# Graph layer, attention and experts on one core: degrees from VectorE's sums, attention stored from GpSimd, transposes moved into the next product

## The chip, the cores and the metric

The program runs on one core of a Trainium2 chip. The metric is the device time of one execution in microseconds, of which the median over several runs is taken.

## What is computed

1250 nodes with 1024 features and 40000 edges go through a layer norm, then side by side through a two-layer graph convolution and a linear-attention block; the sum with the input goes through a second layer norm and a mixture of eight experts. Cut to the parts that matter here:

```python
x = x + positional_encoding
deg = segment_sum(ones, dst) + 1.0
dinv = deg ** -0.5
h = gcn_conv(x, W1, b1)                     # x @ W1, gathered by src, summed by dst, scaled by dinv[src]*dinv[dst]
h = relu((h - mean) * rsqrt(var + eps) * gamma + beta)
h = relu(gcn_conv(h, W2, b2))
attn = linear_attention(xn, Wq, Wk, Wv, proj) @ Wo + bo
x = x + h + attn
x = x + experts(layernorm(x))
```

## The kernel before, in words

Every engine has its own program, and all of them walk the same list ORDER, made by steps(). A key of the list, such as ("O", 3), is one unit of work; each engine does its share of it and skips keys that don't concern it. Semaphores psum_full, act_done and dve_done count the units that TensorE, ScalarE and VectorE have finished; an engine that needs a unit waits for its number. SP issues nearly all DMAs, also in the order of ORDER, so a wait for one holds back all behind it. GpSimd issues the additions into adj_d and, late in the program, the experts' gathers and scatters.

float32 products are made of float32r parts: a matrix is split in a high and a low part (ScalarE copies the high part, VectorE subtracts), and three products are summed. Two PSUM areas, slot0 and slot1, take the results in turn; free_slot() makes TensorE wait until the last user of a slot has been read.

The stages around the change, in order:

- **The adjacency counts.** During the attention stage groups of 500 edges are turned into small blocks of counts, which GpSimd adds into adj_d in DRAM, one addition after the other. When the last is in, GpSimd raises adj_complete (L834).
- **Eight blocks O 0 to 7** (slab_product, L1785): the output projection of the attention, 72 products of 418 columns for each block of 128 output features. ScalarE evicts a block to mixt with the bias (L958). Inside the next block, after the third of eight steps kt, TensorE transposes mixt by ten transposes (mix_transposes, L1712, key OT); VectorE copies the result to mixn (L1444); SP stores mixn to mix_d as 1250 rows of 512 B (key OT, L595). mixn has one buffer for the first seven blocks, so the copy of block f waits for the store of block f - 1. OT f stands in the slot that O f + 2 needs. Between them SP loads adj_d in three thirds of 418 columns (key RL and RP 0, tile raw, 125 rows of 4180 numbers each, two buffers), and ScalarE and VectorE copy each third, one half each, into adj as float32r (RP 0 to 2, L896 and L1302), at O 3, 4 and 5.
- **DG** (L1842), between O 5 and O 6: 30 products of ones with adj (ten row tiles by three thirds) give the degree of every node on all 128 partitions. VectorE takes the maximum with 1, ScalarE the root (L951), VectorE the reciprocal and a Newton step (DN, L1310), and ten small transposes (DT) give the same with nodes on partitions.
- **Z 1**: eight blocks of 60 products with adj (L1857), the first layer's aggregation.
- **Eight blocks H 0 to 7** (slab_product again): the first layer's product. ScalarE evicts with the bias to htmp (L989, semaphore h_biased), VectorE takes mean and variance, ScalarE applies them with the relu (L994). Then key HT: ten transposes of htmp (L1874), ScalarE copies to hout, SP stores it to h_d. HT f - 1 comes after H f in the list, as a unit of its own.
- **Z 2** with h_d, the second product (N), and the experts.

Of the kernel before, what the change touches and what calls it, by code (L numbers as in the profile page):

```python
# [17 lines left out]
F32R = mybir.dt.float32r  # L18
# [5 lines left out]
ALU = mybir.AluOpType  # L24
# [4 lines left out]
T = 125  # L29
# [63 lines left out]
def steps():  # L93
# [55 lines left out]
    for layer in (1, 2):  # L149
# [14 lines left out]
        for f in range(KD if layer == 1 else 0):  # L164
            o += with_split(("H", layer, f))
            if f == 4:
                o.append(("ZP", 2, 0))
            if f:
                o.append(("HT", f - 1))
# [22 lines left out]
INNER |= {("FT", i) for i in range(NT - 1)}  # L192
# [84 lines left out]
def build(nc, x, src_cols, dst_cols, dst_groups, slabs, wv, w1, w2, wr, proj, feat_rows, consts, turns, tie,  # L277
          iota, keys, eye, pe, blank, before, list_blank, tokens, expert_at, b2_rows, out):
    ctx = ExitStack()
    with ctx:  # L280
# [28 lines left out]
        def at(name, off, shape, dt=F32):  # L309
            return nc.alloc_sbuf_tensor_at(name, shape, dt, offset=base + off)  # L310
# [38 lines left out]
        mixt = at("mixt", R + 75776, [128, NP])  # L349

# [240 lines left out]
        def _(sp):  # L591
# [68 lines left out]
            for k in ORDER:  # L660
# [78 lines left out]
                elif k[0] == "OT":  # L739
                    f = k[1]  # L740
                    sp.wait_ge(dve_done, DVED[k])
                    spread(mix_d.rearrange("(j p) (f c) -> f p j c", p=T, c=128)[f], mixn[f // (KD - 1)][:, :, :],
                           mix_stored[f // (KD - 1)])
# [51 lines left out]
        def _(pool):  # L795
# [38 lines left out]
            pool.sem_inc(adj_complete, 1)  # L834

# [301 lines left out]
        def _(dve):  # L1137
# [111 lines left out]
            for k in ORDER:  # L1249
# [48 lines left out]
                elif kind == "RP":  # L1298
# [3 lines left out]
                    dve.tensor_copy(adj[:, NT // 2:, o:o + CW], raw[h % 2][:, :, NT // 2:].rearrange("p d j -> p j d")  # L1302
                                    ).then_inc(dve_done, 1)
# [306 lines left out]
        def _(ten):  # L1610
# [94 lines left out]

            def mix_transposes(f):
# [63 lines left out]
            def slab_product(k, ps):  # L1770
# [5 lines left out]
                for kt in range(KD):  # L1776
# [11 lines left out]
                    if kt == 2 and k[0] == "O" and k[1]:  # L1788
                        mix_transposes(k[1] - 1)
                    if kt == 1 and k[0] == "Q" and k[1]:  # L1790
                        attention_product(("AT", k[1] - 1, 1))
# [8 lines left out]
            for k in ORDER:  # L1800
# [35 lines left out]
                if kind == "DG":  # L1836
# [3 lines left out]
                    for j in range(NT):  # L1840
                        for q in range(3):
                            mm = ten.matmul(ps[:, 512 * q:512 * q + CW], ones_r[:T, :], adj[:, j, CW * q:CW * q + CW],  # L1842
                                            start=(j == 0), stop=(j == NT - 1))
# [26 lines left out]
                elif kind == "HT":  # L1870
                    src_t = htmp[k[1] % 2]
                    ten.wait_ge(act_done, ACTED[("H", 1, k[1])])
                    for j in range(NT):
                        mm = ten.transpose(ps[:T, 128 * j:128 * j + 128], src_t[:, T * j:T * j + T], ident[:, :])  # L1874
# [238 lines left out]
```

## Time and profile before

| | |
|---|---|
| Runs | 1512.24, 1513.09, 1516.08 us; median 1513.09 us |
| Profiled execution | span of 1512.1 us; its time isn't listed apart from the runs |
| TensorE | busy 1420.6 us, 94%, 7718 products |
| VectorE, ScalarE | 852.9 us (56%), 533.1 us (35%) |
| GpSimd | 185.5 us (12%) |
| DMA | 194.34 MB, 129 GB/s; q1 (issued by SP) 32.8% of 16 engines, q0 (issued by GpSimd) 17.5% |
| Mean granted TensorE clock | 0.983 of full speed |

Times count from the start of the span. In a row of the chain of waits stand start, length and what held the end back; in a timeline row start, length, engine, line, instruction and in brackets the idle time ahead of it with its releaser; in a DMA row packets, MB and the time of the packets as a share of 16 engines.

### The profile page before, as it was taken

How to read it: one execution, taken by the hardware profiler on the slowest of the kernel's cores; microseconds unless marked ns; L12 is line 12 of the kernel's file. 1: busy time of each engine (PE TensorE's matmuls, PEld its weight loads, DVE VectorE, ACT ScalarE, POOL GpSimd, SP SyncE). 2: the span in 40 equal slices, each digit the busy share in tenths (PEclk: the TensorE clock that was granted, in tenths of full speed). 3: DMA queues.
4: the chain of work that ended last, by engine and by line, in shares of the span. 5: the costliest groups of instructions: out<-in, count | busy, mean ns of one | idle time of the engine just before them, and what ended most of it. 6: DMA issues, size and time to landing. Idle time of an engine off the chain costs nothing.

```text
span 1512.1 us, 20042 instructions
## 1 busy us (share of the span) xinstructions
PE 1420.6 (94%) x7718; PEld 1305.8 (86%) x7718; DVE 852.9 (56%) x1563; ACT 533.1 (35%) x621; POOL 185.5 (12%) x182
## 2 busy tenths in 40 slices
PE   6999899999999999899999999999999849999995
PEld 5888889998998899899999999999788648888884
DVE  7464677777777787733656323355567744443340
ACT  4233344354344444423122133322111234544441
POOL 0111210110100101000000000000001442223311
PEclk9999999999999999999999999999999959999998
DMA  9765433232431434868353033221655578887863
GB/s 307 238 163 113 74 52 77 44 79 51 71 76 30 98 72 109 299 153 206 86 147 90 15 87 103 90 88 32 167 164 164 141 216 201 212 221 179 195 152 77
DMA packets 97187, 194.34 MB, mean 129 GB/s; under 512 B 31715, under 2 KB 62426, under 8 KB 95373
## 3 DMA queue, kind: packets, MB, share of 16 engines
q1 hardware_dynamic: 76324, 145.83, 32.8%
q0 software_dynamic: 20768, 47.22, 17.5%
q8 instruction: 62, 1.02, 0.3%
q14 instruction: 33, 0.27, 0.1%
HBM read 129.78 MB, written 73.13 MB: 134 GB/s over the span
## 4 chain that ended last, share of the span: by engine, by line
PE 70%; DMA 12%; DVE 9%; ACT 5%; issue 2%; SPq 1%; POOL 0%; POOLq 0%; ACTq 0%; DVEq 0%
PE slot L1785 24%; PE slot L1857 12%; PE slot L2014 7%; DMA adj_d<-stage 6%; PE slot L1982 6%; PE slot L1944 5%; PE kvb L2014 3%; PE kvb L1897 3%; DMA xn_d<-dx 2%; PE slot L1741 2%; PE slot L1882 2%; DVE qp_l L1415 1%; PE slot L1997 1%; DMA mix_d<-mixn 1%; PE slot L1919 1%
## 5 line engine op out<-in xcount | busy, mean ns | idle before, releaser
L1785 PE MATMUL slot<-big_hi,slab_h 128*128 128x418 f32 x768 | 195.2, 362 | 14.7 <-DVE qp_l L1415 9.2
L1785 PE MATMUL slot<-big_lo,slab_h 128*128 128x418 f32 x768 | 189.0, 354 | 0.0
L1785 PE MATMUL slot<-big_hi,slab_l 128*128 128x418 f32 x768 | 187.7, 352 | 0.0
L1785 PEld LDWEIGHTS slot<-big_hi,slab_h 128*128 128x128 f32 x768 | 139.3, 189 | 21.8 <-DVE qp_l L1415 12.5
L1785 PEld LDWEIGHTS slot<-big_hi,slab_l 128*128 128x128 f32 x768 | 144.8, 189 | 2.4
L1785 PEld LDWEIGHTS slot<-big_lo,slab_h 128*128 128x128 f32 x768 | 144.7, 189 | 2.0
L816 POOL DMA_DIRECT2D adj_d<-stage x80 | 67.3, 842 | 499.6 <-ACT stage L896 340.4
L1857 PE MATMUL slot<-adj,xs_h 125*128 125x418 f32 x480 | 118.2, 354 | 0.8 <-DVE ztmp L1147 0.5
L1857 PE MATMUL slot<-adj,xs_l 125*128 125x418 f32 x480 | 117.4, 352 | 0.0
L1151 DVE TENSOR_SCALAR oh_src<-lane,src_lo 125x125 bf16<-125x125 f16 x320 | 83.4, 261 | 35.2 <-PE kvb L1640 21.2
L841 POOL DMA_INDIRECT list_d<-rec,spots x20 | 27.9, 1397 | 529.1 <-issue 511.7
L1857 PEld LDWEIGHTS slot<-adj,xs_h 125*128 125x128 f32 x480 | 90.4, 189 | 2.2 <-DVE ztmp L1147 0.7
L1857 PEld LDWEIGHTS slot<-adj,xs_l 125*128 125x128 f32 x480 | 90.5, 189 | 1.2
L1151 DVE TENSOR_SCALAR oh_key<-key_iota,key_rel 125x240 bf16<-125x240 int16 x320 | 90.2, 282 | 0.0
L1147 DVE TENSOR_TENSOR ws_l<-ws_raw,ws_h 128x1024 fp32r<-128x1024 f32 x32 | 38.9, 1219 | 85.6 <-ACT ws_h L896 85.6
L1429 DVE RECIPROCAL nrm<-nrm 128x1254 f32<-128x1254 f32 x8 | 63.9, 7993 | 33.3 <-ACT nrm L896 33.3
L1147 DVE TENSOR_TENSOR slab_l<-slab_raw,slab_h 128x1024 fp32r<-128x1024 f32 x34 | 41.5, 1220 | 55.3 <-ACT slab_h L896 55.3
L876 POOL DMA_INDIRECT out_dram<-y,lists x32 | 49.1, 1533 | 180.7 <-ACT y L896 175.0
L1398 DVE SCALAR_TENSOR_TENSOR kk_l<-slot,kk_h 125x512 fp32r<-125x512 f32 x80 | 51.6, 686 | 26.3 <-ACT kk_h L1029 25.8
L2014 PE MATMUL slot<-xe_h,ws_h 128*128 128x420 f32 x176 | 64.4, 366 | 2.0 <-DVE xe_l L1147 2.0
L1029 ACT ACTIVATE kk_h<-slot 125x512 fp32r<-125x512 f32 x80 | 45.9, 596 | 52.8 <-PE slot L1882 52.3
L2014 PE MATMUL slot<-xe_l,ws_h 128*128 128x420 f32 x176 | 63.0, 358 | 0.0
(316 smaller groups left out, 2939.0 us busy)
## 6 DMA issues: line engine op xcount, KB each, us to landing
slab_raw<-slabs_dram SPq DMA_DIRECT2D x40, 512.0 KB, 3.9
ws_raw<-w_dram SPq DMA_DIRECT2D x36, 512.0 KB, 7.9
adj_d<-stage POOLq DMA_DIRECT2D x81, 117.2 KB, 3.1
w_raw<-w_dram SPq DMA_DIRECT2D x9, 1024.0 KB, 7.7
adj_d<-eye_dram POOLq DMA_DIRECT2D x1, 6250.0 KB, 24.3
raw<-adj_d SPq DMA_DIRECT2D x3, 1828.8 KB
dx<-x_dram SPq DMA_DIRECT2D x10, 448.0 KB
xn_d<-dx SPq DMA_DIRECT2D x10, 448.0 KB
```

Source lines behind the costliest of these rows:

```text
L816: pool.dma_start(adj_d[:, bass.ds(first, SPAN), :].rearrange("p d j -> p (d j)"), stage[g % 3][:, :], accum_op=ALU.add).then_inc(e_added, 16)
L876: pool.indirect_dma_start(out, bass.IndirectOffsetOnAxis(ap=lists[:, e, i, 0:1].bitcast(U32), axis=0), y[i][:, :], None, compute_op=ALU.ad ...
L1029: act.activation(kk_p[k[2] % 3][0][:, :], kk_bank(k), ACT.Relu).then_inc(act_done, 1)
L1147: return dve.tensor_tensor(o, a, b, op)
L1151: dve.tensor_scalar(o, a, s1, None, op0)
L1398: dve.scalar_tensor_tensor(out=kk_p[k[2] % 3][1][:, :], in0=kk_bank(k), scalar=0.0, in1=kk_p[k[2] % 3][0][:, :].bitcast(F32), op0=ALU.max, ...
L1429: link(dve.reciprocal(nrm[:, :], nrm[:, :]))
L1785: mm = ten.matmul(ps[:, 512 * q:512 * q + CW], w[a][:, kt, :], big[b][:, kt, CW * q:CW * q + CW], start=(kt == 0 and c == 0), stop=(kt == ...
L1857: mm = ten.matmul(ps[:, 512 * q:512 * q + CW], xs_p[t % 2][a][:, j, :], adj[:, j, CW * q:CW * q + CW], start=(j == 0 and a == 0), stop=(j ...
L1944: mm = ten.matmul(ps[:T, 512 * q:512 * q + 512], big[b][:, kt, T * i:T * i + T], rows_p[kt][a][:, 512 * q:512 * q + 512], start=(kt == 0 a ...
L1982: mm = ten.matmul(to[:RT_, 512 * q:512 * q + 512], a_p[a][:, f, RT_ * i:RT_ * i + RT_], w2_p[e % 2][b][:, f, 512 * q:512 * q + 512], start ...
L2014: mm = ten.matmul(ps, w[a][:, kt, :], xe[b][:, kt, :], start=(kt == 0 and c == 0), stop=(kt == KD - 1 and c == 2))
```

## The change

Three things are changed.

1. VectorE sums the ten numbers of every column of raw right behind its copy of that third, into a new tile deg_part (125 x 418, three of them); DG multiplies ones with the three tiles, three products in place of 30. dve_done for RP comes after the sum.
2. SP no longer stores mixn. GpSimd does, in one loop of eight steps, which stands after adj_complete in its program.
3. HT 0 to 6 stand ahead of H 1 to 7 in ORDER, and TensorE makes their transposes inside the H block, after the fifth of the eight steps kt. HT is now in INNER, so that it takes the slot of its own H block; H blocks take the slots in turn.

```diff
@@ -162,11 +162,9 @@
             if layer == 2 and t == 1:
                 o.append(("P", ROWS_AT + 1))
         for f in range(KD if layer == 1 else 0):
-            o += with_split(("H", layer, f))
+            o += with_split(("H", layer, f), [("HT", f - 1)] if f else [])
             if f == 4:
                 o.append(("ZP", 2, 0))
-            if f:
-                o.append(("HT", f - 1))
     o += [("P", ROWS_AT + 6), ("P", ROWS_AT + 7)]
     in_front = {6: [("RT", 0), ("RK", 0)], 7: [("PX", 0), ("RW", 0), ("RX", 0), ("SL", 0)],
                 8: [("RT", 1), ("RK", 1), ("RW", 1), ("RX", 1)], NT - 1: [("NA", NT - 1)]}
@@ -189,7 +187,7 @@
 
 ORDER = steps()
 INNER = {("XT", i) for i in range(1, NT)} | {("AT", p, 1) for p in range(PAIRS - 1)}
-INNER |= {("FT", i) for i in range(NT - 1)}
+INNER |= {("FT", i) for i in range(NT - 1)} | {("HT", f) for f in range(KD - 1)}
 AMID = {(6, 3): ("RT", 0), (7, 3): ("PX", 0), (8, 1): ("RT", 1), (8, 6): ("PX", 1)}
 PSUM_KINDS = {"DG", "DT", "Z", "H", "HT", "XT", "V", "K", "Q", "KK", "QP", "AT",
               "O", "OT", "N", "FT", "R", "RT", "PX"}
@@ -347,6 +345,7 @@
 
         raw = [at(f"raw{s}", R + (50176, 80896)[s], [T, CW, NT]) for s in range(2)]
         mixt = at("mixt", R + 75776, [128, NP])
+        deg_part = [at(f"deg_part{h}", R + (66912, 68608, 97632)[h], [T, CW], F32R) for h in range(3)]
 
         turn_no = at("turn_no", R + 45280, [128, NG])
         xw = [at(f"xw{n}", R + 66912 + 320 * n, [128, NG]) for n in range(4)]
@@ -736,11 +735,6 @@
                             load_att(t)
                         sp.wait_ge(att_stored, 32 * (PAIRS - 1))
                         load_att(p)
-                elif k[0] == "OT":
-                    f = k[1]
-                    sp.wait_ge(dve_done, DVED[k])
-                    spread(mix_d.rearrange("(j p) (f c) -> f p j c", p=T, c=128)[f], mixn[f // (KD - 1)][:, :, :],
-                           mix_stored[f // (KD - 1)])
                 elif k == ("N", 0):
                     sp.wait_ge(psum_full, FULL[("Z", 2, KD - 1)])
                     sp.wait_ge(dve_done, DVED[("Z", 2, KD - 1)])
@@ -832,6 +826,11 @@
                 pool.wait_ge(x_added, r * 16 + 16)
                 pool.sem_inc(x_ended, 1)
             pool.sem_inc(adj_complete, 1)
+            for f in range(KD):
+                pool.wait_ge(dve_done, DVED[("OT", f)])
+                for part in ROWS:
+                    pool.dma_start(mix_d.rearrange("(j p) (f c) -> f p j c", p=T, c=128)[f][part],
+                                   mixn[f // (KD - 1)][part]).then_inc(mix_stored[f // (KD - 1)], 16)
 
             pool.wait_ge(list_cleared, 16)
             for c, (a, b) in enumerate(CHUNKS):
@@ -1299,8 +1298,10 @@
                     h = k[1]
                     dve.wait_ge(raw_landed[h % 2], LAND * (h // 2 + 1))
                     o = CW * h
-                    dve.tensor_copy(adj[:, NT // 2:, o:o + CW], raw[h % 2][:, :, NT // 2:].rearrange("p d j -> p j d")
-                                    ).then_inc(dve_done, 1)
+                    dve.tensor_copy(adj[:, NT // 2:, o:o + CW], raw[h % 2][:, :, NT // 2:].rearrange("p d j -> p j d"))
+                    with nc.allow_low_precision(reason="sums of counts"):
+                        dve.tensor_reduce(deg_part[h][:, :], raw[h % 2][:, :, :], AX.X, ALU.add
+                                          ).then_inc(dve_done, 1)
                 elif kind == "DG":
                     dve.wait_ge(psum_full, u)
                     ts(chunks(ztmp[0][:, :]), cols(ps), 1.0, ALU.max).then_inc(deg_ready, 1)
@@ -1703,6 +1704,13 @@
                                     start=False, stop=(j == b - 2), skip_group_check=True)
                 mm.then_inc(psum_full, 1)
 
+            def hidden_transposes(f, ps):
+
+                ten.wait_ge(act_done, ACTED[("H", 1, f)])
+                for j in range(NT):
+                    mm = ten.transpose(ps[:T, 128 * j:128 * j + 128], htmp[f % 2][:, T * j:T * j + T], ident[:, :])
+                mm.then_inc(psum_full, 1)
+
             def mix_transposes(f):
 
                 free_slot(("OT", f))
@@ -1787,6 +1795,9 @@
                                             start=(kt == 0 and c == 0), stop=(kt == KD - 1 and c == 2))
                     if kt == 2 and k[0] == "O" and k[1]:
                         mix_transposes(k[1] - 1)
+                    if kt == 4 and k[0] == "H" and k[2]:
+                        free_slot(("HT", k[2] - 1))
+                        hidden_transposes(k[2] - 1, sums[SLOT[("HT", k[2] - 1)]])
                     if kt == 1 and k[0] == "Q" and k[1]:
                         attention_product(("AT", k[1] - 1, 1))
                     if kt == KD - 1:
@@ -1837,10 +1848,9 @@
                     for h in range(3):
                         ten.wait_ge(act_done, ACTED[("RP", h)])
                         ten.wait_ge(dve_done, DVED[("RP", h)])
-                    for j in range(NT):
-                        for q in range(3):
-                            mm = ten.matmul(ps[:, 512 * q:512 * q + CW], ones_r[:T, :], adj[:, j, CW * q:CW * q + CW],
-                                            start=(j == 0), stop=(j == NT - 1))
+                    for q in range(3):
+                        mm = ten.matmul(ps[:, 512 * q:512 * q + CW], ones_r[:T, :], deg_part[q][:, :],
+                                        start=True, stop=True)
                 elif kind == "DT":
                     ten.wait_ge(deg_ready, 1)
                     for j in range(NT):
@@ -1868,10 +1878,8 @@
                     slab_product(k, ps)
                     continue
                 elif kind == "HT":
-                    src_t = htmp[k[1] % 2]
-                    ten.wait_ge(act_done, ACTED[("H", 1, k[1])])
-                    for j in range(NT):
-                        mm = ten.transpose(ps[:T, 128 * j:128 * j + 128], src_t[:, T * j:T * j + T], ident[:, :])
+                    hidden_transposes(k[1], ps)
+                    continue
                 elif kind == "KK":
 
                     p, i = k[1], k[2]
```

SP's queue, from the blocks O 0 and O 1 on. Before:

```order
L715 DMA slab_raw_51<-slabs_dram 128x1024 [waits dve_done]
L595 DMA mix_d<-mixn_137 112x10x128 [waits dve_done]
L595 DMA mix_d<-mixn_137 13x10x128
L595 DMA raw_107<-adj_d 112x4180 [waits dve_done,adj_complete]
L595 DMA raw_107<-adj_d 13x4180
L595 DMA raw_108<-adj_d 112x4180
L595 DMA raw_108<-adj_d 13x4180
L715 DMA slab_raw_52<-slabs_dram 128x1024 [waits dve_done]
L595 DMA mix_d<-mixn_137 112x10x128 [waits dve_done]
L595 DMA mix_d<-mixn_137 13x10x128
```

GpSimd's queue with the change, from the last addition into adj_d on:

```order
L824 DMA adj_d<-stage_104 125x240
L826 ISA
L820 REGISTER_ALU [waits x_added]
L820 COMPARE_AND_BRANCH
L832 DMA mix_d<-mixn_140 112x10x128 [waits dve_done]
L832 DMA mix_d<-mixn_140 13x10x128
L832 DMA mix_d<-mixn_140 112x10x128 [waits dve_done]
L832 DMA mix_d<-mixn_140 13x10x128
```

The first store stood ahead of the loads of raw; it now stands behind the last addition into adj_d, for which the loads of raw wait too. The others leave SP's queue.

VectorE around the second third of raw, with the change (before, the row of L1303 isn't there):

```order
L1146 TENSOR_TENSOR slab_l_56<-slab_raw_52,slab_h_55 128x1024 [waits act_done]
L1301 CAST adj<-raw_108 125x5x418 [waits raw_landed1]
L1303 TENSOR_REDUCE deg_part_111<-raw_108 125x418
L1445 COPY mixn_140<-slot 125x1280 [waits mix_stored0,psum_full]
L1146 TENSOR_TENSOR slab_l_54<-slab_raw_51,slab_h_53 128x1024 [waits act_done]
```

The sum stands between the copy of the third and the copy of mixn.

TensorE at the transposes of the first hidden block, H 0. Before, between H 1 (slab_55) and H 2 (slab_53):

```order
L1785 MATMUL slot<-big_hi,slab_h_55 128x418 x3
L1785 MATMUL slot<-big_lo,slab_h_55 128x418 x3
L1785 MATMUL slot<-big_hi,slab_l_56 128x418 x3
L1874 MATMUL slot<-ident,htmp_132 125x128 [waits act_done,h_biased]
L1874 MATMUL slot<-ident,htmp_132 125x128 x9
L1785 MATMUL slot<-big_hi,slab_h_53 128x418 [waits dve_done,h_biased]
L1785 MATMUL slot<-big_hi,slab_h_53 128x418 x2
```

With the change:

```order
L1793 MATMUL slot<-big_hi,slab_h_55 128x418 x3
L1793 MATMUL slot<-big_lo,slab_h_55 128x418 x3
L1793 MATMUL slot<-big_hi,slab_l_56 128x418 x3
L1711 MATMUL slot<-ident,htmp_135 125x128 [waits act_done,h_biased]
L1711 MATMUL slot<-ident,htmp_135 125x128 x9
L1793 MATMUL slot<-big_hi,slab_h_55 128x418 x3
L1793 MATMUL slot<-big_lo,slab_h_55 128x418 x3
```

The transposes now have products of H 1 on both sides, and the wait for h_biased no longer stands at the start of H 2.

## Rows read from the trace of the kernel before

**Rows 1.** The page, part 4: the chain that ended last, shares by engine.

```profile
PE 70%; DMA 12%; DVE 9%; ACT 5%; issue 2%; SPq 1%; POOL 0%; POOLq 0%; ACTq 0%; DVEq 0%
```

**Rows 2.** Waits of TensorE, 634 to 1090 us: total, times, longest.

```profile
PE slot L1785 <- DVE mixn L1444: 2.2, 1, 2.2
PE slot L1785 <- ACT htmp L989: 1.8, 6, 0.3
```

**Rows 3.** Chain in order of time, 634 to 765 us: start, length, what.

```profile
658.92 3.11 DMA adj_d<-stage
...
665.20 21.50 DMA mix_d<-mixn
...
694.88 13.79 PE slot L1785 x72
708.67 1.09 PE slot L1712 x10
...
718.38 5.74 PE slot L1842 x30
```

**Rows 4.** TensorE's timeline, 634 to 765 us: start, length, instruction, idle before.

```profile
671.12 0.74 PE L1785 MATMUL slot<-big_hi,slab_h 128*128 128x418 f32 x3
...
688.34 0.84 PE L1785 MATMUL slot<-big_hi,slab_h 128*128 128x418 f32 x3 [2.19 <-DVE mixn L1444]
```

**Rows 5.** VectorE's timeline, 634 to 765 us.

```profile
706.97 2.51 DVE L1302 CAST adj<-raw 125x2090 fp32r<-125x2090 f32 x1
709.80 1.49 DVE L1444 COPY mixn<-slot 125x1280 f32<-125x1280 f32 x1 [0.33 <-PE slot L1712]
```

**Rows 6.** VectorE's groups by shape: count, busy us, mean ns of one.

```profile
L1166 DVE TENSOR_REDUCE gmm<-grp_f 80x1 f32<-80x500 f32 x1 | 0.7, 669 | 0.0
...
L1519 DVE TENSOR_REDUCE rank<-cmp_gt 125x32 f32<-125x256 f32 x1 | 0.4, 420 | 0.0
```

**Rows 7.** ScalarE's timeline, 634 to 765 us.

```profile
718.42 1.31 ACT L958 ACTIVATE mixt<-slot,rows 128x1254 f32<-128x1254 f32 x1 [8.58 <-PE slot L1785]
```

**Rows 8.** DMA queue, 674 to 678 us: packets, MB, share of 16 engines.

```profile
q1 hardware_dynamic: 66, 1.10, 95.9%
```

**Rows 9.** DMA queues, 40 to 44 us.

```profile
q0 software_dynamic: 26, 1.30, 97.0%
q1 hardware_dynamic: 27, 0.11, 10.3%
```

**Rows 10.** DMA queue, 1187 to 1192 us.

```profile
q0 software_dynamic: 96, 0.01, 7.3%
```

**Rows 11.** DMA queue, 655 to 662 us.

```profile
q0 software_dynamic: 144, 0.12, 16.0%
```

**Rows 12.** DMA queues, 88 to 89 us.

```profile
q0 software_dynamic: 113, 0.10, 70.1%
q1 hardware_dynamic: 59, 0.17, 43.4%
```

**Rows 13.** Busy time by engine, granted clock (1.00, 0.68), DMA; 1198 to 1204 us.

```profile
1198.00:1203.00 5.00, 1.82 (x15) 1.42 (x13) 4.19 (x17) 1.36 (x4) 0.00 (x0) 1.00 0.21 60
1203.00:1204.00 1.00, 0.28 (x2) 0.19 (x2) 0.90 (x7) 0.98 (x2) 0.00 (x0) 0.68 0.84 283
```

**Rows 14.** Chain in order of time, 1060 to 1260 us.

```profile
1236.55 6.82 PE slot L2014 x24
...
1244.10 4.61 PE slot L2014 x24
```

**Rows 15.** Chain in order of time, 845 to 990 us.

```profile
849.46 27.55 PE slot L1785 x144
...
878.39 14.06 PE slot L1785 x72
...
971.05 11.75 PE slot L1857 x60
```

**Rows 16.** ScalarE's timeline, 845 to 1000 us.

```profile
913.22 1.44 ACT L994 ACTIVATE htmp<-htmp,bsc 128x1254 f32<-128x1254 f32 x1 [1.78 <-DVE bsc L1147]
```


## The prediction

> **What bounds the kernel now.** I read the page's chain by engine first: TensorE holds 70% of it, DMA 12% [rows 1]. A product that is removed is therefore worth its time only where TensorE has no other wait there, so I went on to TensorE's own waits in the stretch that the change touches, the eight output-projection blocks O 0 to 7, the eight hidden blocks H 0 to 7 and what lies between. They are few [rows 2]: one wait of 2.2 us for a copy of mixn, six of 0.3 us for ScalarE's eviction of a hidden block. The chain in order of time shows what stands behind the first: the store of the second transposed column block, from mixn to mix_d, takes 21.50 us from issue to landing [rows 3]. It was issued on SP's queue right behind two loads of raw. VectorE may not overwrite mixn before it lands, and block O 4 cannot start before VectorE has emptied its slot. TensorE's timeline has O 3 at 671.12 and O 4 at 688.34 [rows 4]. A block with transposes inside takes 13.79 + 1.09 = 14.88 us [rows 3], so O 4 was due at 686.00: **2.3 us lost**.
>
> **Degrees.** The 30 products with ones took 5.74 us [rows 3], and nothing covers them. Three remain: 3 x 5.74 / 30 = 0.6 us. But the block behind them, O 6, uses the slot from which ScalarE still evicts O 5. That eviction starts 0.04 us after O 5 ends (718.38) and takes 1.31 us [rows 3, 7]; it was hidden under the 30 products and is now what ends last. The pause shrinks from 5.74 to about 1.4 us: **-4.35 us**.
> VectorE pays with three reductions of 4180 numbers a lane. The two rows of 500 and 256 numbers give (669 - 420) / 244 = 1.02 ns a number, the second with groups of eight [rows 6], so 669 + 3680 x 1.02 = 4.4 us each. Around block O 5 the cast ends at 709.48 [rows 5]; with the reduction 713.9, with the copy of mixn behind it 715.4, while the slot is wanted at 718.4. A margin of 3.0 us hides all three; it would be gone at 7.4 us a reduction. Before DG the third one has the same margin. Cost: 0.
> What follows DG on VectorE (the maximum, the reciprocal of 8 us, the small Newton steps) keeps its distance to the start of O 6, because it hangs on transposes inside O 6. I take the later waits as unchanged.
>
> **Hidden transposes.** From the start of H 0 (849.46) to that of the next product (971.05) are 121.59 us [rows 15]: two blocks of 13.78 and then six times a stop for ten transposes, the eviction wait and a new start. Inside a block they cost what they cost inside an O block: 13.78 + 7 x 14.88 = 117.94. **-3.65 us.** The condition is that the normalised block is ready when the fifth of eight steps ends, 8.6 us into the next block. ScalarE's last activation ends at 914.66 [rows 16], 5.4 us after the start of that block (878.39 + 2 x 15.44 = 909.27). Cover: 3.2 us. ScalarE's copy to hout comes later than its preparation of the next slab; both fit before the next eviction.
>
> **The stores.** Leaving SP's queue takes the store of 21.50 us from behind the loads of raw, and the loss of 2.3 us goes: **-2.3 us**. But GpSimd's program has the stores behind adj_complete, and the last addition to adj_d lands only at 658.92 + 3.11 = 662.03 [rows 3]. The very first store, which SP issued as soon as its copy was made, some 12 us before, now starts at 662.4, in the same moment as two loads of raw (2 x 125 rows of 4180 numbers, 4.2 MB) on the other queue. The late store is thus not gone; it is one block earlier: the second copy of mixn waits for it, and O 3, due at 671.12, waits for that copy.
> When does it land? A row of raw is 16.7 kB; 66 packets in 4 us over 16 engines are 0.97 us a row [rows 8], some 16 rows an engine, until about 679. The other overlap of large and small rows is at 40 to 44 us: 26 rows of 50 kB on q0, 27 small packets on q1 [rows 9]. So the queues take turns, packet for packet, whatever their size. The store has 1250 rows of 512 B, 78 an engine. All hangs on how many rows one turn holds. Three indirect stores of 125 elements left 96 packets, 32 each [rows 10]; with 16 of them completions, a data packet holds eight elements. With eight rows a turn the store needs 9 + 2 turns, 10.7 us, on top of the 3.1 us that a small store takes [rows 3]: 662.6 + 3.1 + 10.7 = 676.4. Copy 1.49 [rows 5]: O 3 starts at 678.0, **+6.9 us**. The bounds are 0 (landed before 669.6) and +17.2 (late as the store of 686.7 was).
> TensorE idle for 6.9 us also costs clock. With 1.8 us of work in 5 us the grant fell from 1.00 to 0.68 in the next one [rows 13], to the lower level of 1.2 GHz; the 24 products that met it took 6.82 us, the same 24 later 4.61 [rows 14]. I add **+2.0 us**; bounds 0 and 2.2.
> The later stores find no 4 MB in front of them: the second (about 678) meets the end of raw, the third one load of raw with some 8 turns left, and each has a block of 14.88 us to land in.
>
> **Sum.** -4.35 - 3.65 - 2.3 + 6.9 + 2.0 = -1.4 us. The profiled execution spans 1512.1 us, its surroundings being within a microsecond, since the runs are 1512.24, 1513.09 and 1516.08; the median lies 1.0 above the span. 1513.1 - 1.4 = **1511.7 us**. 0.3%, 4.5 us, is about what a measurement of this kernel can tell from no change.
>
> **Rivals.**
> 1. *Short turns, slower.* A Pool store of 125 rows of 960 B left 144 packets, one for each row [rows 11]. It adds to memory, which the new store doesn't, but it is the nearest direct store of rows. At one row a turn the store has had 16 of its 78 turns when raw ends; it lands where the late one did, at 686.7, and O 3 starts at 688.3: +17.2 + 2.0 - 10.3 = +8.9, **1522 us**. This decides above a landing at 682.6 (stall over 12.9 us gives +4.5). Against it: at 88 to 89 us q0 had 113 packets to 59 on q1 [rows 12], more than one for one. Chance 0.27. The Trainium skill (DMA: Bandwidth & Descriptors, Issuing engines are not separate DMA queues) says that DMAs of all engines end on the same sixteen and interleave, so that a second issuer saves little more than issue time. By that rule the first store would fare as SP's late one did, which is this rival. Rows 9 agree with the interleaving; they also show that a small packet of the other queue isn't kept behind the whole load.
> 2. *Long turns, faster.* If a turn holds a dozen rows or more, or q0 gets two turns for one, five or six turns do: 662.6 + 3.1 + 5.5 = 671.2, O 3 at 672.8, stall 1.7 us, no loss of clock: -8.6; with all rows of an engine in two turns there is no stall, -10.3. **1502.8 to 1504.5 us.** Rows 12 speak for it, rows 11 against. Chance 0.30. The Trainium skill (the same page, Queues, rings and completion order) has the engine take turns at packets and calls 9 to 17 descriptors typical, 64 the most. With 13 of 512 B in a turn it would be this rival. Its section SWDGE vs HWDGE vs iDMA prefers packets of at most 4096 B from GpSimd, eight rows, which would be the forecast. No row here shows the packet of a plain store of short rows, so neither moves the chances.
> 3. *VectorE becomes the bound*: a reduction above 7.4 us delays O 5 and O 6 by the excess. Rows 6 speak against it; up to 3 us, within the range. Chance 0.03.
> The forecast itself has 0.40, and its own range is 1508 to 1516 us: eight-row turns with a landing between 673 and 680 (descriptors that GpSimd needs longer to write, completions, the loss of clock or not).
>
> **Numbers.** Faster by over 4.5 us: rival 2 whole and a twelfth of the rest, 0.35. Slower by over 4.5: rival 1 but for its milder part, 0.24. Within: 0.41. The range leaves out the tails of both rivals: 1503 to 1520.5.
>
> **What would show it.** Three products of L1852 and a start of O 6 about 1.4 us behind O 5. Seven groups of transposes inside H blocks at a spacing of 14.9 us, no waits for htmp. Reductions of 4.4 us. On the path, in place of the wait at 688, one of TensorE just behind 671 for the copy of mixn, which itself waits for the DMA mix_d<-mixn from GpSimd's queue, and a granted clock of 0.5 for some microseconds behind it. Whether q0 shows some 170 or some 1270 packets for that store tells rivals 1 and 2 from the forecast. I am wrong if the first store lands before 669 or after 683, or if the degree part returns less than 4 us because something other than the eviction holds O 6.

## The result, and the profile after

| | before | after |
|---|---|---|
| Median of 20 runs each, side by side | 1514.16 us | 1518.78 us |
| Ratio, 95% interval | | 1.003, 1.0019 to 1.0041 |
| Span of the profiled execution | 1512.1 us | 1513.9 us |
| Mean granted TensorE clock | 0.983 | 0.979 |

The change makes the kernel 4.6 us **slower**; the forecast had the change 1.4 us faster. In the page's chain by engine TensorE and the DMA keep their shares (70 and 12% [rows 1]):

```profile
PE 71%; DMA 12%; DVE 8%; ACT 4%; issue 2%; SPq 1%; POOL 0%; POOLq 0%; ACTq 0%; DVEq 0%
```

The waits of TensorE, 634 to 1090 us, name the place. The wait for mixn of 2.2 us [rows 2] has become one of 13.4, and the six short ones for htmp are gone:

```profile
PE slot L1793 <- DVE mixn L1445: 13.4, 1, 13.4
PE slot L1793 <- ACT mixt L957: 1.0, 2, 0.8
```

The chain of the same stretch in order of time (start, length, what):

```profile
657.51 3.12 DMA adj_d<-stage
...
661.54 0.94 POOL mix_d L832
662.48 19.15 DMA mix_d<-mixn
...
681.72 1.50 DVE mixn L1445
...
683.27 6.80 PE slot L1793 x27
...
720.92 8.63 PE slot L1793 x45
...
729.57 1.32 ACT mixt L957
...
730.93 5.45 PE slot L1793 x27
```

GpSimd issues the first store when the last addition is in. The store is two DMAs, one of 112 rows of mixn and one of 13; the chain shows the second, which takes 19.15 us from its issue to its landing, and O 3, which TensorE reached at 669.87 (683.27 - 13.4), starts at 683.27. O 6 starts 1.38 us after the end of O 5 (720.92 + 8.63 = 729.55), behind ScalarE's eviction, where it was 5.74 us [rows 3].

The DMA queues while the store is under way, 662.4 to 681.7 us, then 662 to 666 and 678 to 682 us (packets, MB, share of 16 engines):

```profile
q1 hardware_dynamic: 389, 4.34, 83.5%
q0 software_dynamic: 208, 0.64, 13.6%
...
q1 hardware_dynamic: 68, 1.14, 97.5%
...
q1 hardware_dynamic: 129, 0.49, 79.5%
q0 software_dynamic: 12, 0.00, 1.2%
```

1250 rows of 512 B went as 208 packets, of which 32 are completions, so up to eight rows in one. In 662 to 666 us there is none of them beside the rows of raw (the first comes at 666.9), and only twelve are left for 678 to 682. The issues of 662 to 666 us (KB, us from issue to landing) tell the two DMAs apart:

```profile
mix_d<-mixn POOLq DMA_DIRECT2D x1, 560.0 KB, 17.0
mix_d<-mixn POOLq DMA_DIRECT2D x1, 65.0 KB, 19.2
```

The first, issued at 661.54, is thus through at 678.6, the small one behind it 3.1 us later (both raise the same semaphore, so the profile tells them apart by the count of completions).

Busy time by engine in four stretches; the column behind the five engines is the granted clock (670 to 672 us, 676 to 682, 683.3 to 685, 685 to 687):

```profile
670.00:672.00 2.00, 0.00 (x0) 0.00 (x0) 0.00 (x0) 2.00 (x2) 0.00 (x0) 1.00 0.89 210
676.00:682.00 6.00, 0.00 (x0) 0.00 (x0) 0.28 (x1) 0.28 (x1) 0.00 (x0) 0.50 0.95 185
683.30:685.00 1.70, 1.70 (x5) 1.63 (x6) 1.70 (x2) 0.00 (x0) 1.49 (x2) 0.50 0.01 2
685.00:687.00 2.00, 2.00 (x9) 1.93 (x8) 2.00 (x2) 0.00 (x0) 1.08 (x1) 0.67 1.03 209
```

The granted clock is still 1.00 in the first two us of the wait and 0.50, the level of 1.2 GHz, at its end. The first 27 products of O 3 take 6.80 us; 27 such products right behind others take 5.16 (969.15 in the chain below): 1.6 us of clock and restart.

VectorE's timeline around the last third of raw, and the chain from H 0 to Z 2:

```profile
718.13 2.51 DVE L1301 CAST adj<-raw 125x2090 fp32r<-125x2090 f32 x1
720.53 4.52 DVE L1303 TENSOR_REDUCE deg_part<-raw 125x418 fp32r<-125x4180 f32 x1
724.94 1.51 DVE L1445 COPY mixn<-slot 125x1280 f32<-125x1280 f32 x1
```

```profile
856.56 22.37 PE slot L1793 x117
878.93 1.09 PE slot L1711 x10
...
968.05 1.09 PE slot L1711 x10
969.15 5.16 PE slot L1793 x27
974.31 11.50 PE slot L1867 x60
```

A sum takes 4.5 us, and the copy behind it ends at 726.45, 3.1 us before the slot is wanted. From H 0 to Z 2 are 974.31 - 856.56 = 117.75 us, 3.84 less than in [rows 15].

The sum of the profiles: from the start of the last 45 products of O 1 (behind its transposes; 647.37 and 645.96 in the chains) to the start of O 6 the program takes 76.75 us before and 84.97 after, +8.2 = 13.4 + 1.6 - 4.36 - 2.5 (the wait of [rows 2] and its restart); O 6 restarts 0.3 us slower, and H gives back 3.84: **+4.6 us**, as the medians say. The spans differ by 1.8 only, since this execution reached O 1 1.4 us earlier and waited 1.3 us less for the experts' gathers (15.0 us and 16.3).

### The profile page after: what moved, and what is told of

Its sections match the earlier page's. It is cut to its first block, busy times and chain, and to the rows that moved or that the text cites. A ratio compares the mean times of both kernels' runs of the same rounds, so it can differ in the third digit from the quotient of the medians.

```text
span 1513.9 us, 19991 instructions
## 1 busy us (share of the span) xinstructions
PE 1414.1 (93%) x7691; PEld 1299.6 (86%) x7691; DVE 865.3 (57%) x1566; ACT 533.5 (35%) x621; POOL 198.3 (13%) x198
## 4 chain that ended last, share of the span: by engine, by line
PE 71%; DMA 12%; DVE 8%; ACT 4%; issue 2%; SPq 1%; POOL 0%; POOLq 0%; ACTq 0%; DVEq 0%
PE slot L1793 25%; PE slot L1867 12%; DMA adj_d<-stage 7%; PE slot L2022 7%; PE slot L1990 6%; PE slot L1952 5%; PE kvb L2022 3%; PE kvb L1905 3%; PE slot L1749 2%; DMA adj_d<-eye_dram 2%; PE slot L2005 2%; PE slot L1890 1%; DVE qp_l L1416 1%; PE slot L1927 1%; DVE kT L1146 1%
## 5 line engine op out<-in xcount | busy, mean ns | idle before, releaser
L1793 PE MATMUL slot<-big_hi,slab_h 128*128 128x418 f32 x768 | 195.8, 363 | 24.9 <-DVE mixn L1445 13.4
L1793 PEld LDWEIGHTS slot<-big_hi,slab_h 128*128 128x128 f32 x768 | 139.6, 190 | 31.2 <-DVE mixn L1445 13.8
```

The costliest lines, as they stand in the source:

```text
L1793: mm = ten.matmul(ps[:, 512 * q:512 * q + CW], w[a][:, kt, :], big[b][:, kt, CW * q:CW * q + CW], start=(kt == 0 and c == 0), stop=(kt == ...
```

## Experiments

The kernels ran in four groups, each beside the kernel before on the same chip. The kernel before took 1515.12 us beside all stores on SP, only the stores, the first store on SP and rows of 4.2 kB; 1513.73 beside the early store on GpSimd, the late one on SP, raw behind the store and the slab behind the store; 1514.0 beside rows of 8.4 kB, short rows in the kernel before, both remedies and only the hidden transposes; 1514.87 beside raw behind the issue and short rows in the kernel before, again. A ratio compares a kernel with the one of its group; where two groups are compared, it is by their ratios. Edits are to the changed kernel unless it says otherwise.

### All stores back on SP

```diff
-            for f in range(KD):                     # GpSimd
-                pool.wait_ge(dve_done, DVED[("OT", f)])
...
+                elif k[0] == "OT":                  # SP, as before
```

> The changed kernel with all eight stores of mixn back on SP's queue, where they stood before; degrees by VectorE and the transposes inside H stay. My theory: the change's loss is the first store's alone. O 3 starts on time again and O 4 has its old loss of 2.3 us; what is left is the degree part (O 6 starts 4.4 us earlier, read from the changed kernel: +11.17 us at the end of O 5, +6.81 at the start of O 6) less 0.3 us of restart, and the hidden transposes (-3.84 us from H 0 to Z 2): 4.36 - 0.3 + 3.84 = 7.9 us faster than before, ratio 0.9948, about 1506.2 us beside 1514.2. Rival 1 (the sums on VectorE delay copies of mixn or slab parts when nothing else holds the blocks back; the long stall of the changed kernel gave them cover): less than 6 us faster, and a new wait at O 4 to O 6. Rival 2 (the changed kernel loses elsewhere too, in the experts): about 4 us faster.

1506.48 us, ratio 0.9949 (0.9929 to 0.9969): the theory's 0.9948. The sums and the hidden transposes are sound, and the loss belongs to the stores. O 4 waits again. The waits of TensorE, then busy time and granted clock during that wait and in the 2 us behind it:

```profile
PE slot L1793 <- DVE mixn L1445: 2.8, 1, 2.8
```

```profile
684.40:687.20 2.80, 0.08 (x1) 0.00 (x0) 1.50 (x2) 2.68 (x3) 0.00 (x0) 0.89 1.24 370
687.20:689.20 2.00, 1.95 (x6) 1.86 (x7) 2.00 (x2) 2.00 (x1) 0.00 (x0) 0.50 0.86 209
```

### Only the stores

The kernel before, with the loop of stores on GpSimd behind adj_complete.

> The kernel before with only the stores of mixn moved to GpSimd, behind adj_complete. My theory: the stall of 13.4 us for the copy of mixn ahead of O 3, 1.5 us of clock behind it, and the old loss of 2.3 us ahead of O 4 gone: +12.6 us, ratio 1.0083, about 1526.8 us beside 1514.2. The first store lands some 19 us after its issue. Rival (the stall is partly made by the sums on VectorE, which stand in the same stretch): the store lands, or its copy is made, some us earlier, and the kernel is under 9 us slower.

1530.07 us, ratio 1.0098 (1.0074 to 1.0122): the interval holds the 1.0083 expected, though the median is 15 us slower and not 12.6. The chain has the same landing without any sum on VectorE:

```profile
668.46 19.50 DMA mix_d<-mixn
```

### Only the first store back on SP

```diff
+                elif k == ("OT", 0):
+                    f = k[1]
+                    sp.wait_ge(dve_done, DVED[k])
+                    spread(mix_d.rearrange("(j p) (f c) -> f p j c", p=T, c=128)[f], mixn[f // (KD - 1)][:, :, :],
+                           mix_first)
...
-            for f in range(KD):
+            for f in range(1, KD):
```

> The changed kernel with the store of OT 0 alone back on SP's queue, where it was issued some 12 us ahead of the loads of raw; the seven others stay on GpSimd. My theory: neither the stall ahead of O 3 nor that ahead of O 4 is left, since the store of OT 1 finds a few turns of raw in front of it and has a block to land in, at worst landing 19 us after its issue at about 663.5, near 682.5, and O 4 is due at 685: -7.9 - 2.3 = -10.2 us, ratio 0.9933, about 1504.0 us beside 1514.2. Rival (any store issued from GpSimd beside the raw loads lands as late as they end, 19 to 22 us after its issue): the second store becomes the late one, O 4 waits up to 2 us, and the kernel is 8 us faster, like the one with all stores on SP.

**1501.56 us, ratio 0.9916** (0.9896 to 0.9935): 12.7 us faster than before, 2.5 more than worked out (perhaps the clock behind the old wait, see below). It is also faster than with all stores on SP (1506.48 in the same group): the second store, issued from GpSimd at 666.9 beside raw, lands after 17.8 us, in time for O 4, where on SP's queue behind raw it was late. No wait for mixn is left in the O blocks; the longest is that of O 6 for ScalarE:

```profile
PE slot L1801 <- ACT mixt L963: 1.0, 2, 0.8
```

### The first store early on GpSimd

```diff
             pool.sem_inc(x_ended, 1)
+            pool.wait_ge(dve_done, DVED[("OT", 0)])
+            for part in ROWS:
+                pool.dma_start(mix_d.rearrange("(j p) (f c) -> f p j c", p=T, c=128)[0][part],
+                               mixn[0][part]).then_inc(mix_stored[0], 16)
             pool.wait_ge(x_counted, 1)
...
-            for f in range(KD):
+            for f in range(1, KD):
```

> The changed kernel with all stores on GpSimd, but the first one ahead of the wait for x_counted and the loop of late additions, so that it is issued as soon as its copy is made, some 12 us ahead of the loads of raw. (This place works only while the loop of late additions runs once, as with these inputs.) It tells the engine apart from the place in its program. My theory: the place is all; no wait for a copy of mixn at O 3 or O 4, and the time is that of the kernel with only the first store on SP, 1501.6 us beside 1515.1, within 2 us. Rival (an eight-row store by GpSimd among the last additions holds those up): adj_complete comes 1 to 3 us later, with it the first third of raw, seen in the start of ScalarE's copy; that would cost little, since RP 0 has some us to spare.

1502.98 us, 0.9926 (0.9901 to 0.9951), and no wait for mixn is left. GpSimd's timeline has the first store 14 us before the second:

```profile
651.19 1.54 POOL L820 DMA_DIRECT2D mix_d<-mixn  x2 [53.31 <-DVE mixn L1449]
...
665.39 1.57 POOL L836 DMA_DIRECT2D mix_d<-mixn  x2 [4.62 <-DVE mixn L1449]
```

Not the engine but the place in its program made the loss.

### The same late start on SP

```diff
+                    sp.wait_ge(dve_done, DVED[("OT", 0)])
+                    spread(mix_d.rearrange("(j p) (f c) -> f p j c", p=T, c=128)[0], mixn[0][:, :, :], mix_stored[0])
                     load_raw(0)
                     load_raw(1)
```

The seven other stores stand on SP's queue as in the kernel before, and GpSimd's loop is gone.

> The changed kernel with all stores on SP's queue, but the first one issued as late as in the changed kernel, when adj_complete is up, directly ahead of the loads of raw. It tells the late start apart from the second queue. My theory: it is not the start behind adj_complete that costs 13.4 us, but that the store shares the engines with packets of 16.7 kB; ahead of them in one queue its 1250 rows need 4 us and it lands at about 669, so that O 3 waits under 1.5 us. The second store then stands behind loads of raw that end 5 us later, lands at 690 to 691, and O 4 waits some 6 us in place of 2.8: about 3 us slower than with all stores on SP at their old place (1506.5), 1510 us. Rival (any start behind adj_complete is too late, since raw loads and store go at once in any case): O 3 waits over 6 us.

1510.45 us, 0.9968 (0.995 to 0.9986). The chain of waits has both stores:

```profile
667.27 3.87 DMA mix_d<-mixn
...
673.12 20.82 DMA mix_d<-mixn
```

Issued as late as GpSimd's, but ahead of raw in one queue, the first store lands in 3.87 us and O 3 waits for nothing. So the late start alone costs nothing either: it takes large rows on the second queue beside the store. The second store, now behind raw, makes O 4 wait 4.7 us.

### Raw behind the store, or behind its issue

```diff
+                    sp.wait_ge(mix_stored[0], LAND)     # first kernel
+                    sp.wait_ge(mix_issued, 1)           # second: GpSimd raises it behind its two issues
                     load_raw(0)
                     load_raw(1)
```

> The changed kernel, but SP issues the two loads of raw only when the first store of mixn has landed, so nothing large stands beside that store. It measures the store by itself. My theory: the 4 us from its issue to its first data packet are GpSimd's own (writing descriptors) and stay; its ten packets an engine then take about 0.25 us each; it lands 7 to 8 us after its issue, at about 670, and O 3 waits 1.5 to 2 us. The loads of raw start 8 us later, the first third lands at about 680 and not 672.4, VectorE's copy and sum of it stand ahead of its copy of OT 2, and O 4 waits 1 to 3 us. In all about 9 us faster than the changed kernel: 1510 us beside 1515 of before. Rival (a store from GpSimd is slow by itself, whatever stands beside it): landing 15 us or more after the issue, O 3 waits over 9 us, and the kernel is slower than the changed one.

1510.61 us, 0.9984 (0.9969 to 0.9999). The chain, and queue q0 in 666 to 670 us:

```profile
666.03 3.78 DMA mix_d<-mixn
...
672.58 18.80 DMA mix_d<-mixn
```

```profile
q0 software_dynamic: 208, 0.64, 59.4%
```

The 208 packets by themselves need 3.78 us, and O 3 waits for nothing. The theory had the first four us of the 19.15 as GpSimd's own; they are not. The second store, now beside raw, inherits the landing of 18.80 us, and O 4 waits 4.6.

> The changed kernel, but SP issues the loads of raw only when GpSimd has issued the first store (not when it has landed), so that the store's packets are in their queues before the first row of raw. My theory: the 4 us until the store's first packet are raw rows that stood before it; they go, the first packet comes within 0.5 us, some of the ten packets an engine are through before raw starts, and the rest take turns with rows of 16.7 kB: it lands 8 to 12 us after its issue, O 3 waits 2 to 6 us in place of 13.4, and the kernel is about 9 us faster than the changed one, near 1508 to 1511 us beside 1514. Rival (the wait for the first packet is no backlog but the price of every first packet beside a busy queue, and the turns take what they took): 15 us or more after the issue, O 3 waits over 9 us, under 4 us faster.

1516.71 us, 1.0014 (1.0005 to 1.0023), some 2 us better than the changed kernel (1.003, 1.0019 to 1.0041; the intervals touch). The chain, then q1 in 663 to 664 us and q0 in 665 to 666:

```profile
662.83 16.77 DMA mix_d<-mixn
```

```profile
q1 hardware_dynamic: 14, 0.23, 121.0%
```

```profile
q0 software_dynamic: 7, 0.03, 9.6%
```

The rival's numbers hold; its reason, a price of every first packet, isn't shown. The store was issued first, but it wasn't first at the engines: rows of raw move from 663.4 us on, and its own first packet comes at 665.5. So this kernel doesn't show what a store would need whose packets really stand ahead of raw. To be issued first takes 2.4 us off, and O 3 waits 11.1; the rest is spent beside raw. (The end of the spread between 676 and 679 us is again 34 packets of next to nothing.)

### The size of raw's rows

```diff
-                spread(raw[h % 2][:, :, :].rearrange("p d j -> p (d j)"),
-                       adj_d[:, CW * h:CW * h + CW, :].rearrange("p d j -> p (d j)"), raw_landed[h % 2])
+                for a, b in ((0, 105), (105, 210), (210, 314), (314, CW)):
+                    spread(raw[h % 2][:, a:b, :].rearrange("p d j -> p (d j)"),
+                           adj_d[:, CW * h + a:CW * h + b, :].rearrange("p d j -> p (d j)"), raw_landed[h % 2])
```

The waits for raw_landed count four times as much.

> The changed kernel as it is, but each load of raw made in four pieces of 104 or 105 columns, so that a row on SP's queue has 4.2 kB and not 16.7 kB; the same bytes in the same order. My theory: a DMA engine takes packets of the two queues in turn, one for one, so the time of the first store hangs on the size of the packets it alternates with. Its ten turns, 11.5 us beside rows of 16.7 kB, take 10 x (0.25 + 0.25) = 5 us; with the 3.5 to 4 us until its first packet it lands at about 672 to 674, and O 3 waits 3 to 6 us and not 13.4: about 8 us faster than the changed kernel, 1510.5 us beside 1514.2 of before. Rival (the bytes of raw, slab and store, 5.4 MB, share the engines' rate, and a store's last packets land when the whole heap does): landing stays at 681, stall 13 us, 1518.8 us. A third way: four times as many issues on SP (some 0.45 us each, 12 more) delay the raw loads by up to 5 us, which RP 0 would show, not O 3.

1505.9 us, 0.9946 (0.9927 to 0.9965), some 13 us less than the changed kernel. Chain and queues (662.4 to 670.1 us):

```profile
662.40 7.68 DMA mix_d<-mixn
```

```profile
q1 hardware_dynamic: 534, 1.86, 76.7%
q0 software_dynamic: 208, 0.64, 23.6%
```

The same 208 packets land after 7.68 us, while raw still runs: it is not the heap of bytes that holds a store back. Nor does it slip into gaps, since the engines are full (76.7 + 23.6%). It lands earlier than the 672 to 674 expected, and O 3 waits 1.8 us.

> The changed kernel with each load of raw in two pieces of 209 columns, rows of 8.4 kB. It gives the third point of one line. My theory: the time from the first store's issue to its landing grows with the duration of the row that it alternates with. Rows of 16.7 kB (0.97 us each) gave 19.2 us, rows of 4.2 kB (0.25 us) 7.7 us, so rows of 8.4 kB (0.49 us) give 7.7 + (19.2 - 7.7) x (0.49 - 0.25) / (0.97 - 0.25) = 11.5 us; O 3 waits 1.8 + 3.8 = 5.6 us, and the kernel is some 5 us slower than with rows of 4.2 kB, about 1510 us beside 1514. Rival (not the size of rows but the number of loads counts, for instance that the 16 loads issued one after the other over 9 us leave the engines gaps, in which the store gets in): with four loads, issued within 4 us, the store lands like that beside two loads, 17 us or more after its issue.

1511.9 us, 0.9984 (0.9974 to 0.9994).

```profile
663.32 13.75 DMA mix_d<-mixn
```

Rows of 4.2, 8.4 and 16.7 kB give 7.7, 13.8 and 19.2 us (11.5 expected for the middle one, 17 or more by the rival): the landing comes later with longer rows on the other queue, though not in proportion. O 3 waits 8.0 us with the middle ones. The number of loads changes with their rows in these runs, so the two are kept apart only by the full engines above.

### The end of the store

```diff
                     load_raw(1)
+                    sp.wait_ge(mix_stored[0], LAND)
```

> The changed kernel, but the load of slab_raw that stands behind the two loads of raw on SP's queue is issued only when the first store of mixn has landed. In the changed kernel the store's last 12 packets fall between 678 and 682 us, where otherwise only that slab's packets of 4 kB move, at 57 to 112 GB/s. My theory: the slab's packets keep the store's last packets waiting for 3 us; without them the store lands at about 678.5, O 3 waits 10.4 us and not 13.4, and the kernel is 3 us faster than the changed one, if the slab is not missed. Rival (the last packets are late for a reason of the store's own, its second part of 13 rows and its completions): landing at 681 to 682 as before, no difference. The slab arrives some 2 us after its need at O 3 in both cases at worst; if so O 4 starts later by that.

1518.69 us, 1.0035 (1.0017 to 1.0053), no gain:

```profile
665.96 19.00 DMA mix_d<-mixn
```

My theory fell: the last packets don't wait for the slab. Its rival named the store's second part of 13 rows, and the record bears that out in part. By the count of completions the second part lands 3.1 us behind the first in the changed kernel and here, 2.3 and 1.4 us behind it beside rows of 8.4 and 4.2 kB, and 0.4 us with nothing beside it. So most of the end is the second DMA, and it too grows with the rows beside it; why the last completions need up to 1.7 us after their packets stays open.

### Short rows in the kernel before, and both remedies together

> The kernel before, with each load of raw in four pieces, rows of 4.2 kB, and nothing else. Here the late store stands behind the raw loads on the same queue, SP's. My theory: in one queue nothing takes turns, the store lands when the raw bytes are through, whatever their rows: no gain, O 4 still loses 2 to 3 us (more, if the nine microseconds in which SP issues 16 loads hold its store back), ratio 1.000 to 1.002. Rival (short rows speed up the raw loads or the store as such, and the gain of the changed kernel with short rows was no matter of two queues): the loss at O 4 goes and the kernel is 2 us or more faster.

1510.74 us, 0.9967 (0.9953 to 0.9981): the theory of one queue fell. The last row of raw starts at 679.7 us before and at 684.3 here, where this execution's loads started 2.4 us later. The queue q1 behind it, 680 to 682 us before and 684 to 686 here:

```profile
q1 hardware_dynamic: 57, 0.10, 62.4%
```

```profile
q1 hardware_dynamic: 1044, 0.71, 109.4%
```

Behind rows of 16.7 kB come two us in which little moves at 62% of the engines; behind short rows the store is already under way. Counted from the first row of raw it lands after 22.3 us and not 23.4. O 4 waits 0.9 us.

> The kernel before with loads of raw in rows of 4.2 kB, the same as before_short_rows, in five rounds and with another profile. My theory: its real gain is what the profile showed in the O blocks, 1 to 2 us (O 4 waits 0.9 us and not 2.2 to 2.8), ratio 0.999, and the 5 us of the first comparison were partly chance. Rival (short rows gain also elsewhere): ratio 0.997 again, and in the profile a stretch outside the O blocks that is 2 us or more shorter than before.

1510.89 us, 0.9971 (0.9962 to 0.9981): the gain of 4.4 us is real, and my 1 to 2 us fell. From O 1 to O 6 this profile shows 74.33 us for 76.75, and no wait at O 4. The two spans differ by no more (1509.6 and 1512.1), so no other stretch gained. The rest agrees with clock that the wait costs in other executions; it was not seen in a profile of before.

> The changed kernel with the store of OT 0 on SP and the loads of raw in rows of 4.2 kB: both remedies at once. My theory: each removes the whole stall, so together they give no more than the first store on SP alone, 1501.6 us beside 1515.1, ratio 0.992, within 0.1%. Rival (the engines are also loaded better with short rows, or SP's 16 issues hold back the slab behind them): 2 us or more off that in either direction, seen as a new wait for slab_h in O blocks, or as fewer waits than now.

1501.7 us, 0.9909 (0.9893 to 0.9926): no more than the first store on SP alone.

### Only the hidden transposes

The kernel before with part 3 of the change.

> The kernel before with the transposes of H 0 to 6 inside the next H block and nothing else. My theory: the stretch from H 0 to Z 2 shrinks by 3.8 us, as in the changed kernel, and nothing else moves: ratio 0.9975. Rival (VectorE or ScalarE, which here have no stall before them that let them run ahead, get late for the slabs in H): less than 2 us.

1510.66 us, 0.997 (0.9955 to 0.9986), as expected. In its profile O 4 waits 2.8 us and then needs 6.97 us for its first 27 products:

```profile
690.57 6.97 PE slot L1790 x27
```

Up to there this is the program of before, whose profile had a wait of 2.2 us and 5.45 for the products: the same code lost 2.1 us more in this execution.

## Why the prediction was wrong, point by point

- **Degrees**, forecast -4.35: measured -4.36, less 0.3 us of restart of O 6 that I had not counted. The sums were forecast at 4.4 us with a margin of 3.0; they take 4.5 with 3.1 left. Right.
- **Hidden transposes**, forecast -3.65: -3.84, no wait for htmp. Right.
- **The late store gone**, forecast -2.3: it is gone. What it had cost isn't settled. The three kernels without any wait for mixn gained 1.0 to 3.6 us more than my sum, and the profile of the kernel with only the hidden transposes shows 4.6 us for it, which speaks for 4 or 5 us. Two results speak against it: the sum of the change itself comes out right with 2.5, and the kernel with only the stores moved, which loses that wait too and should be less slow the more the wait had cost, was 2.4 us slower than expected.
- **The first store**: the mechanism was right, with the copy of mixn as the wait at O 3, eight rows in a packet and the clock at its lower level. The term "10.7 us, on top of the 3.1 us that a small store takes" failed: 13.8 us against 19.15. The eleven turns (9 + 2, one share for each of the two DMAs) took about 12 us (666 to 678), which was nearly well sized, in part by luck: the 0.97 us of a row alone stood for the whole turn, and the store's own packets came on top (some 21% of the engines' time in these 12 us). But no packet comes in the first four us, where the 3.1 us of a small store were meant to hold start and end together, and the end takes three to four more. That price was read from a store with nothing large beside it, and alone this store too needs only 3.8. Another 1.2 us look like an earlier O 3, due at 669.87 and not 671.12; in truth this execution ran 1.4 us ahead, the last addition's landing too (660.63 for 662.03), and GpSimd needed 1.9 us from there to the end of its first issue (662.48), where the forecast had 0.6. 6.9 + 5.3 + 1.2 = 13.4 us. The landing at 681.6 lies past the forecast's own range (up to 680) and short of its sign of being wrong (after 683).
- **Clock**, forecast +2.0: +1.6.
- **Rival 1** (one row a turn) had the wrong mechanism, 208 packets and not 1270, and a size that lies nearer. Its threshold, a stall of 12.9 us for +4.5, was met by 13.4. The Trainium skill's sentence that DMAs of several engines interleave on the same sixteen (DMA: Bandwidth & Descriptors, Issuing engines are not separate DMA queues) agrees with all runs: beside or behind large rows the store takes some 20 us in place of 4, whichever engine issued it. Its second half, that a second issuer saves little more than issue time, doesn't fit: with seven stores on GpSimd the kernel takes 1501.56 us, with all on SP 1506.48. Its preference for packets of at most 4096 B from GpSimd (the same page, SWDGE vs HWDGE vs iDMA) agrees with 0.64 MB in 208 packets.
- **Rival 2** (long turns) fell; so did **rival 3**: 4.5 us a sum.

The gains came to 10.4 us, for 10.3 forecast, and the loss was sized at 8.9 where it is 15: a landing at 681.6, in the later half of the bounds (669.6 to 686.7), turned the sign. The step that failed is the size of the first store's wait, and in it the start and the end of a store that has large rows beside it.

## What to carry to other kernels

A small transfer that frees a buffer should not be put beside large rows on another queue: what counted here is how long the packets last with which it takes turns, so move it ahead of them in time or in their own queue, or cut their rows. Issuing it first on another queue is not enough. When a queue is relieved, look where the moved work stands in its new program: here seven of eight stores were well placed and the first one, behind a wait that it had nothing to do with, cost more than the others gained.

## What the runs showed of the hardware

- A store of 640 kB lands 3.8 us after its issue by itself on GpSimd's queue, 3.9 ahead of raw on SP's, and 7.7, 13.8 and 19.2 beside rows of 4.2, 8.4 and 16.7 kB on the other queue.
- Its first packet comes 0.6 us after the same issue by itself, 2.6 beside rows of 4.2 kB or when issued before rows of 16.7 kB, and 4.7 and 4.4 beside rows of 8.4 and 16.7 kB. This start is not explained.
- From GpSimd's queue the 1250 rows of 512 B went as 208 packets with the completions, from SP's as one packet a row: in the kernel before, 665.2 to 686.8 us, 1356 packets under 2 KB, 106 of them under 512 B, which leaves 1250.
- The clock that a stall costs does not grow with it. The first 27 products of a block, 5.16 us back to back, took after a wait of TensorE of:

| wait, us | 0.9 | 1.8 | 2.2 (before) | 2.8 | 2.8 (all on SP) | 4.6 | 4.7 | 8.0 | 11.1 | 13.2 | 13.4 | 13.7 |
|---|---|---|---|---|---|---|---|---|---|---|---|---|
| 27 products, us | 5.42 | 6.97 | 5.45 | 6.97 | 8.19 | 7.43 | 6.97 | 8.04 | 7.54 | 6.80 | 6.80 | 6.92 |

  The wait of the kernel before got through at a granted clock of 1.00 in its profile; in others one of 1.8 to 2.8 us was followed by means of 0.50 to 0.67 (0.50 is the level of 1.2 GHz) for 2 us or more, which can cost as much as the wait. That may be why its removal gave more than its length in some kernels; only these profiles speak for it, and the sums named above against it.
